# Mixture attention: value product with the values on the loaded side, and the reciprocal row sum folded into the gate weights

## The reference, cut to what matters

```python
n1 = _layernorm(x, ln1_w, ln1_b)
rw = _gating(n1.reshape(b * t, c), smha_sim, smha_gates, MIN_ATT).reshape(b, t, -1)
q = jnp.einsum('btc,ech,bte->bth', n1, q_proj, rw)
k = jnp.einsum('btc,ech,bte->bth', n1, k_proj, rw)
v = jnp.einsum('btc,ech,bte->bth', n1, v_proj, rw)
scale = 1.0 / jnp.sqrt(jnp.asarray(q.shape[-1], q.dtype))
scores = jnp.einsum('bth,bsh->bts', q, k) * scale
scores = jnp.where(causal, scores, -jnp.inf)
attn = jnp.einsum('bts,bsh->bth', jax.nn.softmax(scores, axis=-1), v)
attn_out = jnp.einsum('bth,ehc,bte->btc', attn, o_proj, rw)
hs = x + attn_out
```

## Time and profile before

| | |
|---|---|
| median of 3 executions | 2947.59 us (2945.6 to 2949.4) |
| span of the profiled execution, first to last recorded instruction | 2944.0 us |
| the profiled execution's own time outside its span | not recorded; the median is 3.6 us above the span |
| PE, PEld | busy 2781.7 us (94%), 2561.1 us (87%) |
| DVE | busy 2237.7 us (76%) |
| ACT, POOL | busy 1860.9 us (63%), 1581.3 us (54%) |
| the mixture attention's turns | 613.4 us (first `turn_a`) to 1387.0 us (last) |

### The profile page before, as it was taken

The page is one execution under the profiler, slowest core; times in us unless marked ns, Lnnn a source line. Parts: engine busy times, 40 slices in busy tenths (PEclk is TensorE's granted clock), DMA queues, the critical chain, the costliest instruction groups (busy, mean ns, idle before and its releaser), DMA issues. The chain is left out here.

```text
span 2944.0 us, 79654 instructions
## 1 busy us (share of the span) xinstructions
PE 2781.7 (94%) x26880; PEld 2561.1 (87%) x26880; DVE 2237.7 (76%) x6196; ACT 1860.9 (63%) x6939; POOL 1581.3 (54%) x1816
## 2 busy tenths in 40 slices
PE   6999999789999999998999999999989999999858
PEld 5888888689999999997899999999988888887446
DVE  6988888877777777776877777777768888888735
ACT  5889999755555555555544444444459999998435
POOL 3666666466676777776322222222216666665666
PEclk9999999999999999999999999999999999999979
DMA  6000000010000000000100000000010000000254
GB/s 228 20 17 15 18 15 15 2 63 11 11 11 11 11 11 11 11 11 17 34 13 13 11 11 11 11 11 11 5 48 16 18 15 18 15 18 2 102 161 144
DMA packets 56480, 88.32 MB, mean 30 GB/s; under 512 B 6958, under 2 KB 42799, under 8 KB 55472
## 3 DMA queue, kind: packets, MB, share of 16 engines
q1 hardware_dynamic: 48848, 66.97, 7.4%
q0 software_dynamic: 6528, 16.92, 1.6%
q10 hardware_dynamic: 864, 1.84, 0.2%
HBM read 58.28 MB, written 28.48 MB: 29 GB/s over the span
## 5 line engine op out<-in xcount | busy, mean ns | idle before, releaser
L679 ACT ACTIVATE L_probs<-bank,L_neg_max 128x128 f32<-128x128 f32 x2048 | 716.8, 402 | 117.7 <-DVE L_neg_max L764 112.9
L679 ACT ACTIVATION_READ_ACCUMULATOR L_probs<-bank,L_neg_max 128x1 f32 x2048 | 497.4, 243 | 0.0
L770 DVE COPY L_probsT<-bank 128x512 f32<-128x512 f32 x512 | 341.5, 686 | 109.5 <-PE bank L549 107.7
L1911 ACT ACTIVATE M_inter<-bank 128x512 f32<-128x512 f32 x256 | 153.3, 599 | 385.5 <-PE bank L69 385.5
L67 PE MATMUL bank<-W_hi,M_nT_hi 128*128 128x384 f32 (+1 forms) x1024 | 369.6, 361 | 8.2 <-DVE M_qkv L1496 4.4
L764 DVE TENSOR_REDUCE L_neg_max<-bank 128x4 f32<-128x512 f32 x512 | 327.7, 682 | 30.5 <-PE bank L539 30.5
L68 PE MATMUL bank<-W_hi,M_nT_lo 128*128 128x384 f32 (+1 forms) x1024 | 346.7, 339 | 0.0
L69 PE MATMUL bank<-W_lo,M_nT_hi 128*128 128x384 f32 (+1 forms) x1024 | 346.7, 339 | 0.0
L1978 DVE TENSOR_TENSOR M_inter_lo<-M_inter,M_inter_hi 128x512 fp32r<-128x512 f32 x256 | 183.9, 718 | 177.8 <-ACT M_inter_hi L1912 173.3
L549 PE MATMUL bank<-constants,L_probs 128*128 128x128 f32 x2048 | 303.8, 281 | 12.7 <-ACT L_probs L679 10.6
L67 PE MATMUL bank<-W_hi,M_inter_hi 128*128 128x256 f32 x1024 | 291.6, 285 | 4.2 <-DVE M_inter_lo L1978 3.0
(11 more groups left out here) (342 smaller groups left out, 9018.4 us busy)
## 6 DMA issues: line engine op xcount, KB each, us to landing
L_ctx_in<-in_ctx SPq DMA_DIRECT2D x64, 256.0 KB, 2.7
M_tile<-M_sorted SPq DMA_DIRECT2D x72, 130.0 KB, 2.5
x_all<-in_x SPq DMA_DIRECT2D x8, 1024.0 KB, 10.0
raw_weights<-in_weights SPq DMA_DIRECT2D x2, 4096.0 KB, 15.7
hs<-M_hs SPq DMA_DIRECT2D x64, 128.0 KB, 1.7
M_hs<-hs SPq DMA_DIRECT2D x31, 256.0 KB, 2.6
raw_weights<-in_weights SPq DMA_DIRECT2D x1, 2048.0 KB, 7.6
M_sorted<-M_fill SPq DMA_DIRECT2D x12, 130.0 KB
```

Source lines behind the costliest of these rows:

```text
L679: last = act.activation(probs[:, k % UNITS, i, :], score_bank[u][:, i, :], ACT.Exp, bias=neg_max[:, u, i:i + 1], scale=-1.0, accum_out=sum ...
L770: dve.tensor_copy(probsT[:, k % UNITS], pT_ps[k % UNITS]).then_inc(pT_ready, 1)
L1911: act.activation(inter[:, e % 2], up_bank[e % 2], ACT.Gelu).then_inc(M.inter_ready, 1)
```

## The change

The value product changes sides. Before, the transposed exponentials were loaded and the values streamed, which gave the result as tokens x head. Now the values are loaded and the transposed exponentials stream, which gives head x tokens directly in bank 1. So `turn_a` and `normalize` go, with the tile `attn`. The division by the row sum is no longer made on the result (there the tokens lie along the free axis now) but on the 8 gate weights of each token: `keep_gate` on ACT becomes `scale_gate` on DVE, which writes `rw * row_scale` to `rw_out`. `sum_scale` and `scale_gate` stand ahead of `gate_last`. `round_a` waits for the value product, and newly for both halves of the output projection of the sequence before.

```diff
         masked, probs, probsT = sb("masked", [P, P]), sb("probs", [P, P]), sb("probsT", [P, P])
-        attn = sb("attn", [P, HID])
...
         aT_ps = S.bank[1][:, 0:P]
-        scores, attn_ps, pT_ps = S.bank[2][:, 0:P], S.bank[2][:, 0:HID], S.bank[2][:, P:2 * P]
+        scores, pT_ps = S.bank[2][:, 0:P], S.bank[2][:, P:2 * P]
...
                 def score(s):
                     pe.wait_ge(M.qkT_ready, s + 1)
-                    wait(pe, M.attn_ready, s)
+                    wait(pe, M.pT_ready, s)
...
                 def times_v(s, b):
                     pe.wait_ge(M.pT_ready, s + 1)
-                    pe.matmul(attn_ps, probsT[:], qkv[:, b, 2 * HID:Q3], start=True, stop=True).then_inc(M.attn_made, 1)
-
-                def turn_a(s):
-                    pe.wait_ge(M.attn_ready, s + 1)
-                    pe.transpose(aT_ps, attn[:], S.ident[:]).then_inc(M.aT_made, 1)
+                    pe.matmul(aT_ps, qkv[:, b, 2 * HID:Q3], probsT[:], start=True, stop=True).then_inc(M.attn_made, 1)
...
-                        if e == 6:
-                            turn_a(s)
...
                 def round_a(s):
-                    act.wait_ge(M.aT_made, s + 1)
+                    act.wait_ge(M.attn_made, s + 1)
                     wait(act, M.o_odd_made, 2 * s)
+                    wait(act, M.o_even_made, 2 * s)
...
-                def keep_gate(s, b):
-                    act.wait_ge(M.gate_ready, s + 1)
-                    wait(act, M.o_even_added, 4 * (s - 1))
-                    act.activation(rw_out[:, b, :], rw[:, b, 0, :], ACT.Copy).then_inc(M.kept, 1)
-
...
-                    keep_gate(s, b)
...
-                def normalize(s):
-                    dve.wait_ge(M.attn_made, s + 1)
+                def scale_gate(s, b):
                     dve.wait_ge(M.recip_done, s + 1)
-                    wait(dve, M.aT_made, s)
-                    dve.tensor_scalar(attn[:], attn_ps, row_scale[:], None, ALU.mult).then_inc(M.attn_ready, 1)
+                    dve.wait_ge(M.gate_ready, s + 1)
+                    wait(dve, M.o_even_added, 4 * (s - 1))
+                    wait(dve, M.o_odd_read, 4 * (s - 1))
+                    dve.tensor_scalar(rw_out[:, b, :], rw[:, b, 0, :], row_scale[:], None, ALU.mult).then_inc(M.kept, 1)
...
                         weigh_even(s + 1, 1 - b, 2)
+                    sum_scale(s)
+                    scale_gate(s, b)
                     if two:
                         gate_last(s + 2, b)
-                    sum_scale(s)
                     if one:
                         weigh_even(s + 1, 1 - b, 4)
-                    normalize(s)
```

More of the change, by code:

```diff
@@ L1163, in mixture_attention @@
                  "turned qkT_ready scored max_ready exp_done recip_done pT_made pT_ready attn_made "
-                 "attn_ready aT_made ahi_ready alo_ready o_even_made o_odd_made o_even_added o_odd_read "
+                 "ahi_ready alo_ready o_even_made o_odd_made o_even_added o_odd_read "
                  "o_odd_added y_ready x_added").split()
```

## The result

The changed kernel takes 2962.73 us (median of 4 executions, 2960.4 to 2966.67) against 2948.01 us before: a ratio of 1.0054, 95% interval 1.0042 to 1.0066. It is slower by 0.5%, where 0.24% faster was forecast. The range (2937.5 to 2950) doesn't hold it; rival A's figure was 2964 us.

What follows compares the result with a forecast made beforehand. PE, never stopping in steady turns, was taken as the bound. 58 x 0.119 + 4 x 0.05 = 7.1 us saved, everything else at nothing: 2947.6 - 7.1 = 2940.5 us, 0.24% less; range 2937.5 to 2950 us.

Steps and rivals of the forecast that it cites:

- rival A: Gate's chain on VectorE loses its place between GpSimd's operations; PE loses 0.28 us a turn net, 2964 us; chance 0.17.
- The step that failed: VectorE, gate's second half: L1086 follows the new product before GpSimd's start at 1006.81, so the new work hides entirely.
- The transpose: `turn_a` on PE goes: 0.119 us saved in each of 58 steady turns, 6.9 us.
- a chain that runs free: VectorE's gate chain ends when it ended before, `weigh_even` of expert 4 no later, leaving the full 7.1 us gain.
- The side swap: Value product on PE with exchanged operands costs nothing, within plus or minus 0.02 us, 1.3 us over the stage.
- The slack of bank 4: At the start of a turn, PE's load for bank 4 has 0.16 us slack; 0.04 us remain, enough but thin.
- rival B: PE comes to wait for bank 4; 0 to 0.08 us a turn of gain left, 2943 to 2947.6 us; chance 0.11.
- `round_a` and `score` at nothing: `round_a`'s added wait is on a product PE issues in slot 5; `score` waits for an earlier event: both cost nothing.
- The two engines' alternation: VectorE's gate chain and GpSimd: whoever starts first holds off the other; followed start by start, L1094 ends at 1008.40 as before.

Runs made afterwards that it cites:

- three buffers: Changed kernel with three gate-weight buffers instead of two, new 128x8 product behind `rest_a`, reciprocal back in its old place: 0.9980 of the kernel before.
- the kernel with the spare product: Kernel before with the reciprocal moved ahead of the gate's second half, plus an unused 128x8 product the next operation waits for: 1.0124 of the kernel before.

## Why the prediction was wrong

**The step that failed.** "L1086 is queued right behind it (starts in this queue lie 0.08 us ahead of the end before)". It isn't: `gate_last` begins with a wait on `kept`, for the product of the very turn, and in the changed kernel that signal comes from the instruction just ahead; so L1086 starts 0.11 us behind that instruction's end and 0.06 us behind the start of GpSimd's next operation. I had costed the waits that the change adds, and not one that was there already and whose signal the change moves. The wait was in the code of the kernel before, in `gate_last`, and the new event behind `kept` was in the diff. Moving it showed the step: with the wait ahead of L1086 that operation takes 0.70 us and a turn 12.56 us, with the wait behind it 0.28 us and 12.19 us.

**What held.** The transpose: 0.119 us a turn forecast, 0.11 us by putting it back, 0.14 us from 12.33 to 12.19. (Of its two distances the second, without the transpose, has a mean of 0.350 us over the 60 turns and not 0.347, so the term should have read 0.116; that is 0.2 us in all.) The gain for a chain that runs free: 7.1 us forecast, and with the wait moved 7.1 us by the medians. That the figures meet so closely is luck: the interval of that ratio goes from 3.6 to 9.0 us, and in the trace the 63 turns are 7.8 us shorter, 8.4 us from those behind the fourth less 0.5 us that the first four lost. The side swap at nothing: 0.9997. The slack of bank 4, thin but enough (rival B): 0.16 us down to 0.03 or 0.04 us, with PE's matmuls in slot 1 no further apart than before. `round_a` and `score` at nothing: the kernels with the moved wait and with three buffers keep both and run at 12.19 us. The two engines' alternation: followed start by start it was right for the moved-wait kernel in each of its four starts. But the rule drawn from it, that whoever starts first holds off the other, isn't general: in the kernel with the spare product L1086 started first and was held.

**Rival A was right, at 0.17 where it deserved more.** It named the place, the engine and the time, 2964 us against 2962.73, though not the wait that brings L1086 there. `weigh_even` of expert 4 comes 0.91 us later (0.91 forecast) and PE's load in slot 7 waits 0.40 us (0.40 forecast), but of that PE's matmuls lost 0.35 us; so a turn lost 0.23 us and not 0.28, some 13 us in the 58 steady turns. The other 2 us lie in the first four turns and the last but one, which the rival had left out: that its total came within 1.3 us is in part luck. The margin that decided it I put at 0.01 to 0.02 us, and took a race won by L1088 as evidence that L1086 would win. A step that hangs on 0.02 us should not carry 0.68 of the chance, and a range that leaves out its other side is too narrow.

## What to carry to other kernels

Where a small operation is put ahead of a chain that alternates with another engine, list the waits at the head of that chain, the old ones first, and ask of each which instruction gives its signal now. Put a wait that guards a buffer on the instruction that overwrites it, not at the head of the function. The price read from a full engine (0.12 us of PE a turn) held here, while the one read from a gap of a few hundredths of a us between two other engines was a coin tossed: give such a one a rival with real weight.

## What the runs showed of the hardware

How much earlier VectorE must start to be ahead of GpSimd differs by operation. In this stage L1086 (one 128x8 input and two per-partition scalars, 0.28 us when free) was free in all 183 cases in which it started 0.13 or 0.14 us ahead (61 in each of three traces: the moved wait, the same again, and with the transpose put back), and held in all 61 in which it started 0.01 or 0.02 us ahead (the spare-product kernel, see its rows above). L1088 (two 128x8 inputs, 0.17 us) was free in all 549 cases at 0.01 or 0.02 us (61 in each of nine traces). So the order of recorded starts isn't the order in which one engine comes to hold off the other; the one race won said nothing of the other.

The new product (one 128x8 input and one per-partition scalar, 0.23 us when free) narrows the gap, by single turns at the two ends of the loop. In seven traces it, or the spare product, started 0.06 to 0.09 us ahead and was free; in four it started 0.04 us ahead and was held, as here (VectorE, GpSimd, moved wait):

```profile
1376.34 0.79 DVE L1505 TENSOR_SCALAR M_rw_out<-M_rw,M_row_scale 128x8 f32<-128x8 f32 x1
```

```profile
1376.38 0.72 POOL L1677 TENSOR_TENSOR M_hs_odd<-M_hs_odd,M_hs_even 128x256 f32<-128x256 f32 x1 [1.35 <-DVE M_hs_even L1526]
```

For L1086 itself nothing between 0.02 and 0.13 us is on record in this stage.

L1086 came 0.11 us behind its signal's instruction in the changed kernel (1015.74 to 1015.85) and 0.04 us behind in the kernel with the spare product (1010.36 to 1010.40), where another wait for the product stands first. Both were too late. Why the two differ stays open.
